# Third attention: the shift by the maxima as six more rows of the score product

## The reference

```python
q = _ln(x @ Wq + bq)                    # 256 queries a batch
k, v = _ln(y_main @ Wk + bk), ...       # 240 main keys
k_dca, v_dca = ...                      # the last 16 keys, with weights of their own
ctx = _attn(q, k, v) + _attn(q, k_dca, v_dca)     # each with its own softmax
return ctx @ Wo + bo
```

## Time and profile before

| what | us |
|---|---|
| median of 3 runs (lowest, highest) | 938.35 (933.8, 938.6) |
| the profiled execution | 932.58 |
| its span | 930.8 |
| PE / VectorE / ScalarE / GpSimd busy in the span | 851.7 / 652.0 / 529.2 / 389.1 |
| the loop of the third attention, first shifted product to last value product | 610.77 to 752.87 |

### The profile page before, as it was taken

How to read it: one execution, slowest core, us unless ns; L and a number is a source line. 1 busy time by engine, 2 the same in 40 slices (tenths; PEclk the granted TensorE clock), 3 DMA queues, 4 the chain that set the end, 5 groups by cost and what they waited for, 6 DMA issues and landing times.

```text
span 930.8 us, 13235 instructions
## 1 busy us (share of the span) xinstructions
PE 851.7 (92%) x4430; PEld 611.3 (66%) x4430; DVE 652.0 (70%) x1242; ACT 529.2 (57%) x1011; POOL 389.1 (42%) x334
## 2 busy tenths in 40 slices
PE   5888999999999999976897999998998889999998
PEld 3566878777878778743543854787987754454746
DVE  6569899989898988787775357667777656443211
ACT  3487778777877787984334455545677663112110
POOL 2136777878787778647557325011000003400000
PEclk9999999999999999997999999999999889999999
DMA  5022000000000000110120201000000004000000
GB/s 172 18 77 93 18 18 17 17 17 17 17 17 17 17 20 1 52 46 1 45 69 7 86 1 34 1 1 1 1 1 1 1 1 144 1 0 1 22 1 23
DMA packets 12587, 25.44 MB, mean 27 GB/s; under 512 B 4296, under 2 KB 8032, under 8 KB 11200
## 3 DMA queue, kind: packets, MB, share of 16 engines
q1 hardware_dynamic: 10288, 21.59, 7.2%
q10 hardware_dynamic: 2256, 3.28, 1.0%
HBM read 23.82 MB, written 1.05 MB: 27 GB/s over the span
## 4 chain that ended last, share of the span: by engine, by line
PE 36%; DVE 12%; ACT 5%; POOL 3%; issue 3%; DVEq 0%; ACTq 0%; POOLq 0%
PE PS L2630 14%; PE PS L2644 7%; PE PS L2814 3%; DVE max_groups L2028 2%; PE PS L2599 1%; DVE stats L1364 1%; PE PS L2417 1%; PE PS L2157 1%; ACT regA L1309 1%; PE PS L2443 1%; ACT regC L1289 1%; PE PS L2582 1%; POOL regA L690 1%; POOL regA L685 1%; PE PS L2798 1%
## 5 line engine op out<-in xcount | busy, mean ns | idle before, releaser
L612 POOL TENSOR_TENSOR X<-X,xn 128x512 f32<-128x512 f32 x62 | 106.8, 1722 | 62.1 <-ACT xn L902 61.1
L571 POOL TENSOR_SCALAR veps<-mv 128x4 f32<-128x4 f32 (+1 forms) x20 | 5.9, 296 | 283.8 <-DVE mv L1369 281.8
L2814 PE MATMUL PS<-regA 128*128 128x128 f32 x512 | 74.9, 294 | 9.3 <-ACT regA L1309 9.3
L926 ACT ACTIVATE regA<-PS,nb,rq 128x256 f32<-128x256 f32 x128 | 72.2, 577 | 11.9 <-DVE regA L1470 11.1
L1493 DVE TENSOR_TENSOR_SCAN regB<-regB 128x1024 f32<-128x1024 f32 x30 | 78.6, 2620 | 0.5 <-POOL regA L690 0.3
L605 POOL TENSOR_TENSOR y<-y,regB 128x1024 f32<-128x1024 f32 x32 | 75.6, 2364 | 5.8 <-DVE regB L1504 5.7
L2814 PEld LDWEIGHTS PS<-regA 128*128 128x128 f32 x512 | 68.2, 207 | 13.2 <-ACT regA L1309 11.9
L2248 PE MATMUL PS<-regA 128*128 128x256 f32 x256 | 66.2, 380 | 4.5 <-DVE qss L1457 4.5
L2226 PE MATMUL PS<-regA 128*128 128x256 f32 x256 | 67.3, 386 | 2.4 <-ACT regA L876 2.2
L1470 DVE TENSOR_SCALAR_CACHE_REDUCE regA<-PS,nrq 128x256 bf16<-128x256 f32 x128 | 56.0, 475 | 19.1 <-PE PS L2226 17.2
L2257 PE MATMUL PS<-regA 128*128 128x256 f32 x256 | 65.7, 379 | 0.0
(11 more groups left out here) (337 smaller groups left out, 2014.1 us busy)
## 6 DMA issues: line engine op xcount, KB each, us to landing
regA<-in_W SPq DMA_DIRECT2D x16, 384.0 KB, 3.1
regB<-in_wg SPq DMA_DIRECT2D x2, 1024.0 KB, 6.5
regB<-in_wu SPq DMA_DIRECT2D x2, 1024.0 KB, 8.2
X<-in_x SPq DMA_DIRECT2D x2, 512.0 KB, 5.2
regC<-in_wg ACTq DMA_DIRECT2D x1, 1024.0 KB, 5.2
regC<-in_wu ACTq DMA_DIRECT2D x1, 1024.0 KB, 8.5
regC<-in_wd ACTq DMA_DIRECT2D x1, 1024.0 KB, 10.5
regB<-in_wd SPq DMA_DIRECT2D x1, 1024.0 KB, 4.8
```

What stands on the lines that cost most here:

```text
L612: pool.tensor_tensor(xt, xt, part, ALU.add).then_inc(x0_add, 1)
L926: act.activation(p0[i][:, q, :], bank(S_BANK + i)[:, q * S:(q + 1) * S], ACT.Exp, bias=nb0[:, i, q:q + 1], scale=rq[par][:, 2 * b + q:2 * ...
L2814: last = pe.matmul(bank(6 + g % 2)[:, at:at + P], pT2[i % 3][:, k, q * P:(q + 1) * P], V2flat[:, v:v + P], start=k == 0, stop=k == 1)
```

## The change

The six values of a head that belong to the shift (three parts, two kinds of key) become six more rows of `qsT`, and six constant rows (-1 for the keys of that kind) become six more rows of `ksT`. One product over 102 rows then gives the shifted scores, and `shiftw` and its product go. `mxT` has to be spread: in `mxT` a row is a part, kind and head, with 256 queries; in `qsT` the heads stand beside each other in one partition. SP does it with six transfers a batch, each of 16 rows of 512 bytes into one partition. The layout of `mxs` puts the head last for this. The first pass of the scores of batch b+1 ends at head 12 instead of 13, and SHIFT2 is 13 instead of 14.

```diff
-        ksT = tA(H2, T, dt=BF16)[0:STK]
+        SHK = STK + 6
+        ksT_all = tA(H2, T, dt=BF16)
+        ksT, key_rows = ksT_all[0:STK], ksT_all[STK:SHK]
...
+        qsT = [v[0:STK] for v in qsT_all]
...
-        shiftw = regC[0:STK, 0:H2 * S // 2].bitcast(BF16).rearrange("p (h k) -> p h k", h=H2)
...
-        mxs = sb("mxs", [P, 2, 3, H2, 2], BF16)
+        mxs = sb("mxs", [P, 2, 3, 2, H2], BF16)
+        mxv = mxs.rearrange("p q s w h -> p s q h w")
...
-            start, end = (3 if b else 2), 13
+            start, end = (3 if b else 2), 12
...
-        COT2, WO2, SHIFT2 = 5, 8, 14
+        COT2, WO2, SHIFT2 = 5, 8, 13
...
             sp.wait_ge(kv2_mm, B)
-            sp.dma_start(regC[0:STK, 0:H2 * S // 2], a["shift"]).then_inc(shift_set, 16)
+            sp.dma_start(key_rows.rearrange("p h t -> p (h t)"), a["shift"].bitcast(BF16)).then_inc(shift_set, 16)
+            for b in range(B):
+                sp.wait_ge(mxT_done, b + 1)
+                for row in range(6):
+                    sp.dma_start(qsT_all[b % 2][STK + row:STK + row + 1, :, :],
+                                 mxT[b % 2][H2 * row:H2 * (row + 1), :]).then_inc(shift_set, 16)
...
                 if h == 0:
-                    pe.wait_ge(mxT_done, b + 1)
+                    pe.wait_ge(shift_set, 16 + 16 * 6 * (b + 1))
...
                 for k in range(2):
                     to = bank(4 + i % 2)[:, k * S:(k + 1) * S]
-                    pe.matmul(to, ksT[:, h, (2 * b + k) * P:(2 * b + k + 1) * P], qsT[b % 2][:, h, :], start=True, stop=False)
-                    last = pe.matmul(to, shiftw[:, h, k * P:(k + 1) * P], mxT[b % 2], start=False, stop=True)
+                    last = pe.matmul(to, ksT_all[0:SHK, h, (2 * b + k) * P:(2 * b + k + 1) * P], qsT_all[b % 2][0:SHK, h, :],
+                                     start=True, stop=True)
...
             maxima(0)
             pe.wait_ge(cleared, 7)
-            pe.wait_ge(shift_set, 16)
```

More of the change, by code:

```diff
@@ L241, in build @@
         tB = carve(regB)
-        qsT, stk = [None, None], [None, None]
-        qsT[0] = tB(H2, S, dt=BF16)[0:STK]
+        qsT_all, stk = [None, None], [None, None]
+        qsT_all[0] = tB(H2, S, dt=BF16)
         stk[0] = tB(2, H2, STK, dt=BF16)
@@ L246, in build @@
         tB(DIM)
-        qsT[1] = tB(H2, S, dt=BF16)[0:STK]
+        qsT_all[1] = tB(H2, S, dt=BF16)
+        qsT = [v[0:STK] for v in qsT_all]
         stk[0], stk[1] = kstk, stk[0]
@@ L2037, in maxima_parts @@
                 link(dve.tensor_copy(mxf[:, :, :, 1].rearrange("p q h -> p h q"), max_groups[:, :, :, MAIN // DCA]))
[L2038 to L2041, removed]
+                link(dve.tensor_copy(mxv[:, 0], mxf[:, :, :, :]))
+                link(dve.tensor_tensor(mxr[:, :, :, :], mxf[:, :, :, :], mxv[:, 0], ALU.subtract))
+                link(dve.tensor_copy(mxv[:, 1], mxr[:, :, :, :]))
+                dve.tensor_tensor(mxv[:, 2], mxr[:, :, :, :], mxv[:, 1], ALU.subtract).then_inc(mxs_done, 1)
             def normalise(b, g):
@@ L2785, in maxima @@
                     last = pe.transpose(bank(0).bitcast(BF16)[0:STK, q * P:(q + 1) * P],
-                                        mxs[:, q].rearrange("p s h w -> p (s h w)"), identb[:, :])
+                                        mxs[:, q].rearrange("p s w h -> p (s w h)"), identb[:, :])
                 last.then_inc(mx_tr, 1)
@@ L2969, in _constants @@
     mask[MAIN - P:, 1] = 1
[L2971 to L2974, removed]
+    key = (np.arange(6) % 2)[:, None] == (np.arange(T) % S >= MAIN)
+    shift = np.tile(np.where(key, -1.0, 0.0), (1, H2)).astype(np.float32)
     pairs = lambda v: (v.view(np.uint32) >> 16).astype(np.uint16).view(np.float32)
```

## The result

The changed kernel takes 948.88 us (median of 4 runs, 945.89 to 952.52) against 938.25: a ratio of 1.0137, with a 95% interval of 1.0109 to 1.0166, some 12.9 us slower (the ratio is taken over all the runs; the two medians alone are 10.6 us apart). I had forecast 941.0, in a range of 934 to 948. The direction was the likelier one among changes that can be measured; the size, and the claim that the time would hardly move, were wrong.

The account below looks back on a forecast made before the run. The prediction took the limit to alternate among PE, ScalarE and VectorE by stretch. Its terms, -4.37 + 4.25 + 0.9 + 2.1 + 0.4 - 0.65, gave +2.6 us, so 941.0 us against a median of 938.35, range 934 to 948.

Parts of the forecast that it names:

- The products: Third attention's loop: 128 score products removed, counted only where PE is full or slow and followed by something waiting; -4.37 us.
- 102 rows: Score products: contracting over 102 rows instead of 96 streams the same 256 columns and costs nothing; 1.4 us at the upper end.
- The layout: VectorE's casts and subtraction writing the maxima in the new order: as many and as small, nothing; at the upper end 0.6.
- The doubling that I kept as a far end: VectorE's casts and subtraction in the new order: were they twice as long, 0.6 us a batch.
- The order: Maxima one head earlier: 1.1 us at batch 0 to 1, 0.4 at 1 to 2, -0.65 at 2 to 3.
- The transfers: Six row transfers: +4.25 us at the loop's start, +0.9 for slow PE there, 1.0 at batch 0 to 1.
- SP's issues: Loop's start: the sixth issue starts 2.26 us after the first, as in an earlier burst; landing takes 2.1 more.
- The cover at the later borders: Transfers cost 1.0 us at batch 0 to 1; at 1 to 2 covered with half a microsecond to spare; 2 to 3 nothing.
- The slow PE: Loop's start: after idling nearly five microseconds PE runs at the 1.2 GHz level; +0.9 us (0 to 3.1).
- the signs that I named: Trace of the changed kernel: PE idle to about 615, issues 0.47 us apart, slow first products, loop some 2.6 us longer.
- every batch start waits and PE restarts slow: Rival, all four batch starts: waits and slow restarts at their upper ends, +9.1 us, 947.4; chance 0.29.
- The sum of +10.2: Total if the skill's fixed cost of about 2.0 us were paid six times in a row, 12 us, at the start.

Follow-up runs that it names:

- no transfers, old order: Changed kernel with the six query rows loaded once from a constant and the first pass ending at head 13 as before; 0.9979 against the kernel before.
- the layout run: Kernel before with only the new layout of the maxima `mxs` and its constant in the same order of rows; 1.0016 against the kernel before.
- order run: Kernel before with only the first pass ending at head 12 and SHIFT2 13, both products and old layout kept; 1.0029 against the kernel before.
- the two runs without transfers: Changed kernel with the six query rows loaded once from a constant, in new order and in old order; 1.0008 and 0.9979 against the kernel before.
- the run without transfers: Changed kernel, new order kept, with the six query rows loaded once from a constant (wrong shift); 1.0008 against the kernel before.

## Why the prediction was wrong, point by point

**The products.** Forecast -4.37 us; measured -3.5 (-6.3 to -0.6; no transfers, old order, against the layout run). Counting only the stretches where PE is full was right: all 128 would have been -14.1. One reading under it was too strong: of ScalarE's 40.7 us of waiting, 19.4 lie in the stretches where PE is full, about half and not most.

**102 rows.** Forecast nothing; two shifted products are in the trace at 0.38 us for two, the length of two products over 96 rows. Right.

**The layout.** Forecast nothing, at most 0.6: the parts became 0.45 us longer a batch, and the run's 1.5 us has an interval that includes none (its profiled loop is no longer than before's). The doubling that I kept as a far end was nearly real for the last subtraction.

**The order.** Forecast 1.1 + 0.4 - 0.65 = +0.85; measured +2.7 (0.7 to 4.9). The mechanism at border 0/1 is in the trace as told: the parts precede L1781, `stack_high` starts late, and the copy comes before exponential 14. From one batch's first exponential to the next one's, the new order is longer by 2.6 us in batch 0 (order run against before) or 1.3 (the two runs without transfers), where I had 1.1; by 1.2 or 1.9 in batch 1, where I had 0.4; and shorter by 0.2 in batch 2, where I had 0.65 (one profile each). At 1/2 a part of the excess shows. ScalarE waits for the transposes ahead of its copy for 0.41 us in the order run, as forecast, but for 1.29 with one product (here in the run without transfers):

```profile
678.85 0.37 ACT L1286 COPY regB<-PS 96x256 bf16<-96x256 bf16 x1 [1.29 <-PE PS L2792]
```

**The transfers: the step that failed.** Forecast 4.25 + 0.9 + 1.0 = 6.15 us; measured 12 (9 to 15 by the ratios, 9.6 to 10.5 in the profiled loops). The mechanism, a wait with everything behind it, was right; its terms were too small.
- *SP's issues.* I took 2.26 us for the sixth from loads that spread over many partitions; these are 0.63 apart, 3.2 in all. The landing, 2.1, was about right (1.98 at the start, 1.84 in the chain above; at 1/2 one took 2.81, of which its issue held SP for 1.5). The start cost 5.3, not 4.25, outside the bounds that I gave (3.85 to 4.75). The missing 0.94 us is nearly the whole error here and at 0/1.
- *The cover at the later borders.* At 0/1 ScalarE's wait was 1.9, not 1.0, and at 1/2 it was 1.4 or 0.2, not 0: the half microsecond that I called a margin was less than the error of the issue term. At 2/3 it was covered, as forecast.
- *The slow PE.* Forecast 0.9, once. PE was slow behind the start and behind 0/1 and 1/2 (3.65, 5.20, 4.95 us in the stretches above), where it had a full share of work. What comes behind the direct waits is 3.5 us by the ratios and 1.9 to 2.3 in the profiled loops. How much of this is the slow PE stays open, and at 0/1 the new order has the low clock without any transfer.

Of the signs that I named, PE was idle until 617.59 and not to about 615, the issues are 0.63 and not 0.47 apart, and the loop is 10.1 and not 2.6 us longer; the slow restart at the start, the waits of exponential 16 and the landing between 1.5 and 3 us came as said.

The rival that named this outcome (every batch start waits and PE restarts slow, +9.1 with a chance of 0.29) had the mechanism but for batch 3, whose first exponential was not late, and was cheap in the same terms. The rule of the Trainium skill, "DMA: Bandwidth & Descriptors", section Rules for kernel authors, to coalesce many small transfers pointed the right way. The sum of +10.2 that I made with a fixed cost comes nearer to the 12.9 than mine, but by luck: six of them in a row would take an estimated 12 us at each border, and the first product here comes 5.2 us after SP's first issue. The landings do overlap, and what queues up is the issue on SP. The Trainium skill, same page, section Anatomy of one DMA, gives that fixed cost of about 2.0 us for transfers issued from GpSimd; the landings of these from SP took 1.84 to 1.98, close to it.

## What to carry to other kernels

Work taken off a full engine is worth only the stretches in which that engine is full; work put in front of a queue in order, with every engine waiting behind it, costs close to its whole length, and perhaps more in the speed at which PE resumes. When a small transfer must replace a product, count the issues and not the bytes, price them from issues of the same shape, and give the queue something of its own to do until they land: here the old order and three heads in the old form turned a loss of 1.4% into a gain of 0.3% (0.06 to 0.53). A cover whose margin is smaller than the uncertainty of the thing it covers is no cover.

## What the runs showed of the hardware

An issue on SP of a transfer of 16 pieces of 512 bytes into one partition holds the queue for 0.59 us (median of 24, where two took 1.15 and 1.54) and mostly comes 0.63 after the one before, from memory and from on-chip alike; most loads before the loop had 0.43. GpSimd issued three in 2.07 us, where SP issued three in 1.88. VectorE's casts of 64 elements to bfloat16 took 0.31 us where two neighbouring results lie 32 bytes apart and 0.20 where they are adjacent, and a subtraction 0.45 against 0.23.
